# ScalarE takes over the normalising of rows in phases 1 to 3 of an eight-block transformer kernel; a late product is moved by one chunk, and the last result goes out in two halves

## What is computed

```
x = x + tanh(g_xattn[0]) * L0_xattn(layernorm(x), ctx)     # phase 0: attention without softmax
x = x + tanh(g_ffn[0])   * L0_ffn(layernorm(x))            # phase 1: MoE, 8 experts, top 2, width 256
x = x + tanh(g_xattn[1]) * L1_xattn(layernorm(x), ctx)     # phase 2: one-head attention ("riding heads")
x = x + tanh(g_ffn[1])   * L1_ffn(layernorm(x))            # phase 3: MoE, 16 experts, top 4, width 128
x = x + tanh(g_xattn[2]) * L2_xattn(layernorm(x), ctx)     # phase 4: 16-head attention
x = x + tanh(g_ffn[2])   * L2_ffn(layernorm(x))            # phase 5: slots and a GRU step
x = x + tanh(g_xattn[3]) * L3_xattn(layernorm(x), ctx)     # phase 6: 16-head attention
x = x + tanh(g_ffn[3])   * L3_ffn(layernorm(x))            # phase 7: MoE, 32 experts, top 8, width 64

def _layernorm(x, axis=-1, eps=1e-05):
    m = jnp.mean(x, axis=axis, keepdims=True)
    v = jnp.var(x, axis=axis, keepdims=True)
    return (x - m) / jnp.sqrt(v + eps)
```

## Time and profile before

| engine | busy us | share | instructions |
|---|---|---|---|
| TensorE products | 821.9 | 95% | 4427 |
| TensorE weight loads (beside the products) | 558.9 | 65% | 4427 |
| VectorE | 519.4 | 60% | 1446 |
| GpSimd | 471.3 | 55% | 449 |
| ScalarE | 405.5 | 47% | 729 |

### The profile page before, as it was taken

How to read it: one execution, slowest core, us unless ns; L and a number is a source line. 1 busy time by engine, 2 the same in 40 slices (tenths; PEclk the granted TensorE clock), 3 DMA queues, 4 the chain that set the end, 5 groups by cost and what they waited for, 6 DMA issues and landing times. The chain is left out here.

```text
span 861.6 us, 13585 instructions
## 1 busy us (share of the span) xinstructions
PE 821.9 (95%) x4427; PEld 558.9 (65%) x4427; DVE 519.4 (60%) x1446; ACT 405.5 (47%) x729; POOL 471.3 (55%) x449
## 2 busy tenths in 40 slices
PE   5999999998899999999998999999999999999997
PEld 5876676665667666665665666666665576666664
DVE  6866645594765737235545868686856748556431
ACT  2443354634536242334767676756565663424231
POOL 5585756466672646575545444353555366565452
PEclk9899999999999999999999999999999999999999
DMA  8303110314313232332234141412123141424251
GB/s 317 100 21 99 49 50 11 107 43 155 111 38 123 74 122 76 124 122 49 72 93 117 28 108 26 112 29 71 40 60 75 25 146 56 149 69 148 76 157 45
DMA packets 44727, 75.29 MB, mean 87 GB/s; under 512 B 8977, under 2 KB 9361, under 8 KB 44529
## 3 DMA queue, kind: packets, MB, share of 16 engines
q1 hardware_dynamic: 44512, 74.42, 28.5%
q10 hardware_dynamic: 144, 0.01, 0.0%
HBM read 56.11 MB, written 1.51 MB: 67 GB/s over the span
## 5 line engine op out<-in xcount | busy, mean ns | idle before, releaser
L1178 POOL TENSOR_TENSOR shared<-shared,bcs 128x512 f32<-128x512 f32 x192 | 247.4, 1292 | 204.0 <-DVE shared L1214 186.7
L1214 DVE TENSOR_TENSOR shared<-shared,B 128x512 f32<-128x512 f32 x204 | 139.6, 687 | 205.5 <-PE B L862 158.8
L1066 ACT ACTIVATE shared<-B 128x512 f32<-128x512 f32 x204 | 121.6, 598 | 273.7 <-PE B L862 273.2
L935 PE MATMUL Y<-shared,down_lo 128*128 128x512 f32 x408 | 208.3, 596 | 0.0
L1723 POOL TENSOR_TENSOR shared_r<-shared_r,const 128x512 fp32r<-128x512 f32 (+1 forms) x128 | 116.5, 940 | 87.2 <-PE B L1483 69.7
L1782 DVE TENSOR_REDUCE mxh<-B 128x4 fp32r<-128x512 f32 (+1 forms) x128 | 78.8, 617 | 78.4 <-PE B L1483 77.6
L1660 ACT COPY shared<-B 128x512 f32<-128x512 f32 (+1 forms) x128 | 64.7, 505 | 61.7 <-PE B L1502 61.7
L1650 ACT ACTIVATE shared<-B 128x512 f32<-128x512 f32 (+1 forms) x128 | 69.6, 543 | 51.1 <-PE B L1489 49.8
L935 PEld LDWEIGHTS Y<-shared,down_lo 128*128 128x128 f32 x408 | 72.2, 189 | 21.1 <-issue 9.5
L860 PE MATMUL B<-shared_r,gate_hi 128*128 128x512 f32 x102 | 80.9, 794 | 0.0
L860 PE MATMUL B<-x_lo_r,gate_hi 128*128 128x512 f32 x102 | 76.2, 747 | 0.4 <-ACT shared L1066 0.4
(11 more groups left out here) (311 smaller groups left out, 1472.0 us busy)
## 6 DMA issues: line engine op xcount, KB each, us to landing
bcs<-wrow SPq DMA_DIRECT2D x96, 256.0 KB, 3.6
shared_r<-shared_r SPq DMA_DIRECT2D x256, 64.0 KB, 2.0
bcs<-wrow SPq DMA_DIRECT2D x128, 128.0 KB, 2.9
gate_lo<-in_moe SPq DMA_DIRECT2D x9, 256.0 KB, 5.4
up_lo<-in_moe SPq DMA_DIRECT2D x9, 256.0 KB, 5.7
down_lo<-in_moe SPq DMA_DIRECT2D x9, 256.0 KB, 4.6
small<-in_small SPq DMA_DIRECT2D x1, 1372.5 KB, 11.7
X<-in_x SPq DMA_DIRECT2D x4, 256.0 KB, 5.2
```

The source lines that it names most:

```text
L935: nc.tensor.matmul(Y[:], w_raw[2][:, at:at + P], hid[(n0 + c) % HIDDEN], start=(i == 0), stop=(i == m["NC"] - 1))\
L1066: nc.scalar.activation(sg[(n0 + n) % ACTIVE], B[n % GATES][:], ACT.Silu).then_inc(sem("sg_ready"), 1)
L1178: gp.tensor_tensor(hid[(n0 + n) % HIDDEN], hid[(n0 + n) % HIDDEN], bcs[(PLACE.k0[p] + r // m["PER"]) % BROADCAST], ALU.mult)\
L1214: nc.vector.tensor_tensor(hid[(n0 + n) % HIDDEN], sg[(n0 + n) % ACTIVE], up[:], ALU.mult)\
```

## The change

1. In `STREAMS[0]` ScalarE normalises the rows of the MoE steps: Identity activations with scale = rstd and bias = offset, tiles 0 and 1 three chunks behind the statistics, tiles 2 and 3 four chunks behind. GpSimd's L1163 is left only in phase 7.
2. The riders' `apply` moves from VectorE to ScalarE, at the same d=3.
3. For both, VectorE writes the negated means as well, and GpSimd multiplies them with rstd behind its power (`offset`, `offset2`).
4. The riders' `out` and `update` move from d=12 to d=13, and on VectorE the riders' steps of a chunk now stand in front of the MoE statistics.
5. The last result is done in two halves of 256 columns on ScalarE, TensorE (two PSUM banks), VectorE and in the store.

```diff
@@ norm_stats
+            if negate:
+                nc.vector.tensor_scalar(neg_mean[:], mv[:, :, 0], -1.0, None, ALU.mult)
             nc.vector.tensor_scalar(var[:], mv[:, :, 1], LN_EPS, None, ALU.add).then_inc(sem("var_ready"), 1)
@@ RIDE
-            pe={1: ("k",), 2: ("v",), 4: ("xt",), 5: ("q",), 6: ("score",), 10: ("turn",), 11: ("av",), 12: ("out",)},
-            act={1: ("k",), 4: ("xt",), 5: ("q",), 7: ("exp",), 10: ("turn",)},
-            dve={0: ("stats",), 2: ("v",), 3: ("apply",), 6: ("max",), 8: ("norm",), 11: ("add_q",), 12: ("update",)},
+            pe={1: ("k",), 2: ("v",), 4: ("xt",), 5: ("q",), 6: ("score",), 10: ("turn",), 11: ("av",), 13: ("out",)},
+            act={1: ("k",), 3: ("apply",), 4: ("xt",), 5: ("q",), 7: ("exp",), 10: ("turn",)},
+            dve={0: ("stats",), 2: ("v",), 6: ("max",), 8: ("norm",), 11: ("add_q",), 13: ("update",)},
@@ ride_act
+            elif what == "apply":
+                act.wait_ge(sem("ride_offset"), g + 1)
+                for j in range(GB):
+                    ins = nc.scalar.activation(xr[:, tiles(j)], token_tile(g, j), ACT.Identity,
+                                               bias=offset2[:, j:j + 1], scale=rstd2[:, j:j + 1])
+                ins.then_inc(sem("ride_xhat"), 1)
@@ ride_dve
+                v.tensor_scalar(neg_mean2[:], mv2[:, :, 0], -1.0, None, ALU.mult)
-            elif what == "apply":
-                dve.wait_ge(sem("ride_rstd"), g + 1)
-                for j in range(GB):
-                    ins = v.tensor_scalar(xr[:, tiles(j)], token_tile(g, j), mv2[:, j, 0:1], rstd2[:, j:j + 1],
-                                          ALU.subtract, ALU.mult)
-                ins.then_inc(sem("ride_xhat"), 1)
@@ ride_pool
                 gp.tensor_tensor(rstd2[:], var2[:], minus_half[:], ALU.pow).then_inc(sem("ride_rstd"), 1)
+                pool.wait_ge(sem("ride_rstd"), g + 1)
+                gp.tensor_tensor(offset2[:], neg_mean2[:], rstd2[:], ALU.mult).then_inc(sem("ride_offset"), 1)
@@ stream_act
+            def apply(s, js):
+                act.wait_ge(sem("offset_ready"), s)
+                for j in js:
+                    ins = nc.scalar.activation(xhat[s % 2][:, j * P:(j + 1) * P], token_tile(s % NG, j), ACT.Identity,
+                                               bias=offset[:, j:j + 1], scale=rstd[:, j:j + 1])
+                if GB - 1 in js:
+                    ins.then_inc(sem("xhat_ready"), 1)
...
+                if run is STREAMS[0] and n in (3, 4):
+                    apply(run.step(1), (0, 1) if n == 3 else (2, 3))
+                for late in (3, 4) if run is STREAMS[0] else ():
+                    H = run.hook("stats", n - late)
+                    if H is not None and run.step(H) + 2 < LAST:
+                        apply(run.step(H) + 2, (0, 1) if late == 3 else (2, 3))
...
-                result_act(act, 7, LAST - 1)
+                act.wait_ge(sem("y_ready"), LAST)
+                act.wait_ge(sem("yt_ready"), LAST - 1)
+                for h in range(2):
+                    cols = slice(2 * h * P, 2 * (h + 1) * P)
+                    nc.scalar.activation(ysb[:, cols], Y[:, cols], ACT.Identity, bias=ybias[:, 7:8],
+                                         scale=tgate[:, 7:8]).then_inc(sem("last_ysb"), 1)
@@ stream_pool
+                if run is STREAMS[0]:
+                    pool.wait_ge(sem("rstd_ready"), s + 2)
+                    gp.tensor_tensor(offset[:], neg_mean[:], rstd[:], ALU.mult).then_inc(sem("offset_ready"), 1)
             def apply(s, js):
+                if run is STREAMS[0]:
+                    return
@@ stream_dve
+                for g, what in run.rides("dve", n):
+                    ride_dve(dve, st, g, what)
                 H = run.hook("stats", n)
                 if H is not None and run.step(H) + 2 < LAST:
-                    norm_stats(st, (run.step(H) + 2) % NG)
-                for g, what in run.rides("dve", n):
-                    ride_dve(dve, st, g, what)
+                    norm_stats(st, (run.step(H) + 2) % NG, run is STREAMS[0])
@@ the end: SyncE, TensorE, VectorE
+            for h in range(2):
+                sp.wait_ge(sem("last_x"), h + 1)
+                c = slice(((NG - 1) * GB + 2 * h) * P, ((NG - 1) * GB + 2 * h + 2) * P)
+                sp.dma_start(out_d[:, c], X[:, c]).then_inc(sem("stored"), 16)
...
+            for h in range(2):
+                pe.wait_ge(sem("last_ysb"), h + 1)
+                for j in (2 * h, 2 * h + 1):
+                    ins = nc.tensor.transpose((T, B[0])[h][:, tiles(j)], ysb[:, tiles(j)], ident)
+                ins.then_inc(sem("last_yt"), 1)
...
-            finish_dve(dve, NG - 1, LAST)
+            for h in range(2):
+                dve.wait_ge(sem("last_yt"), h + 1)
+                x = X[:, ((NG - 1) * GB + 2 * h) * P:((NG - 1) * GB + 2 * h + 2) * P]
+                nc.vector.tensor_tensor(x, x, (T, B[0])[h][:, 2 * h * P:2 * (h + 1) * P], ALU.add).then_inc(sem("last_x"), 1)
```

More of the change, by code:

```diff
@@ L195, in build @@
         rstd = sb("rstd", [P, GB])
+        neg_mean = sb("neg_mean", [P, GB])
+        offset = sb("offset", [P, GB])
         minus_half = sb("minus_half", [P, GB])
@@ L229, in context, with norm_stats @@
             return CT[:, g * TG + j * P:g * TG + (j + 1) * P:step]
-        def norm_stats(st, g):
+        def norm_stats(st, g, negate=False):
             for j in range(GB):
@@ L560, in build @@
         k2, q2, v2, pr2, pn2, pt2, aq2, xr, xr_t = (area1.tile([P, TG]) for _ in range(9))
-        mx2, nb2, rs2, ri2, var2, rstd2 = (sb(n, [P, GB]) for n in ("mx2", "nb2", "rs2", "ri2", "var2", "rstd2"))
+        mx2, nb2, rs2, ri2, var2, rstd2, neg_mean2, offset2 = (
+            sb(n, [P, GB]) for n in ("mx2", "nb2", "rs2", "ri2", "var2", "rstd2", "neg_mean2", "offset2"))
         mv2 = sb("mv2", [P, GB, 2])
@@ L1198, in stream_dve @@
             if run is STREAMS[0]:
-                norm_stats(st, 1)
+                norm_stats(st, 1, True)
                 pieces = iter(())
@@ L2052, in _ @@
                 moe_sp(sp, 7, g)
-            for g in range(NG):
+            for g in range(NG - 1):
                 sp.wait_ge(sem("x_updated"), LAST - NG + 1 + g)
@@ L2056, in _ @@
                 sp.dma_start(out_d[:, c], X[:, c]).then_inc(sem("stored"), 16)
-            sp.wait_ge(sem("stored"), 16 * NG)
+            for h in range(2):
+                sp.wait_ge(sem("last_x"), h + 1)
+                c = slice(((NG - 1) * GB + 2 * h) * P, ((NG - 1) * GB + 2 * h + 2) * P)
+                sp.dma_start(out_d[:, c], X[:, c]).then_inc(sem("stored"), 16)
+            sp.wait_ge(sem("stored"), 16 * (NG + 1))
         @block.gpsimd
@@ L2112, in _ @@
             pe.wait_ge(sem("x_updated"), LAST - 1)
-            pe.wait_ge(sem("ysb_ready"), LAST)
-            for j in range(GB):
-                ins = nc.tensor.transpose(T[:, j * P:(j + 1) * P], ysb[:, j * P:(j + 1) * P], ident)
-            ins.then_inc(sem("yt_ready"), 1)
+            for h in range(2):
[3 more added lines that the diff above has]
+                ins.then_inc(sem("last_yt"), 1)
         @block.vector
```

## The result

The changed kernel takes 851.8 us (median of 4 runs, 849.3 to 853.8) against 863.2 us: a ratio of 0.988, interval 0.985 to 0.991. The prediction said 849.8 us, range 846.8 to 857.5. The profiled execution took 851.25 us (span 849.5) where that of before took 863.39 (span 861.6), 12.1 us less instead of 13.6. The ratio lies clear of the 0.5% that a measurement can tell, though the gain is under 2%.

A forecast was written before the change was run, and what follows sets the result against it. TensorE's work was taken as the kernel's length, its waits as removable: 5.7 (riders' transposes) + 4.3 (last products) + 3.2 (clock) + 0.4 (tail) = 13.6 us, so 863.4 - 13.6 = 849.8 us, range 846.8 to 857.5.

The forecast's parts named there:

- What bounds the kernel: TensorE, busy 821.9 of 861.6 us, sets the length; its waits in phases 1 to 3 can go.
- Part 1: Riders' normalising on ScalarE: TensorE's waits at their transposes shrink from 6.1 us by 5.7.
- Part 2: GpSimd's new 128x4 multiply for the offset: 0.2 us each, upper end 1.03, no cost to the kernel.
- Rival A: Third rider's offset comes 4 us late from GpSimd's queue, ScalarE is held; 855.3 us, chance 0.20.
- Part 4: Riders' last product one chunk on: waits of 4.8 us shrink by 4.3, 0.55 stays at the third.
- Part 5: Both stretches at 1.2 GHz behind the two long waits go, 1.6 us each, 3.2 us in all.
- Part 6: Last result in halves at the kernel's end: 0.4 us saved, ends 0.15 and 0.6.
- Rivals B and C: B: MoE-step Silus held behind the offset, 867.8 us, chance 0.06. C: waits return at other products, 859.7, 0.07.
- the 3.0 us of room: At the MoE tiles, a Silu ending at 298.51 is needed by its gate product only at 301.53.
- VectorE's new negations ... Nothing: 12 small VectorE instructions, none ahead of a product TensorE waits for: cost 0, or 1 us if one slips.

The follow-up runs named there:

- e1: Kernel before with only the riders' normalising moved to ScalarE, with its negated mean and offset; 856.05 us, ratio 0.994.
- e3: Changed kernel with the MoE norm put back on GpSimd, tile by tile; 853.26 us, ratio 0.990.
- e4: Kernel before with only the MoE norm tiles moved to ScalarE; 862.27 us, ratio 1.000.
- e6: Changed kernel with the last product and update of the third and fourth rider yet one chunk later; 851.52 us in one execution.
- e9: Changed kernel with the last three weight splits of phase 3 one or two chunks later; 849.25 us in one execution.
- e8: Changed kernel with five extra activations, each waited for, ahead of the third rider's tiles on ScalarE; 858.46 us in one execution.
- e2: Kernel before with only the riders' last product and update one chunk on, ahead of VectorE's MoE statistics; 859.82 us, ratio 0.996.
- e7: Changed kernel with two extra activations, each waited for, ahead of the third rider's tiles on ScalarE; 853.53 us in one execution.
- e11: The kernel of e9 again, timed in rounds against the kernel before; 851.35 us, ratio 0.989.

## Why the prediction was right, and what it missed

- **What bounds the kernel.** Right. TensorE's products are the same, and the time went where its waits were named.
- **Part 1, the riders' rows.** 5.7 us expected, 5.95 found. At the third rider 0.2 us was to be left and 0.21 is. The reason was not quite the one given. The transposes stand 1.64 us earlier than before; in before's time ScalarE was free at 196.60 as expected (196.62), but the offset was ready at 196.68, not 196.0. The activations, 1.65 instead of 1.85 us, made that good.
- **Part 2, GpSimd's multiply.** 0.2 us expected, 0.20 and 0.27 found; the upper bound of 1.03 could go. Rival A had its mechanism right: e1 shows it at 1.1 us. The removed tiles keep it away, as the argument against it said; e3 puts 1.4 us on them. e4 shows a second way in which they act, by which of GpSimd's long instructions stand beside VectorE's.
- **Part 4, the last product.** 4.3 expected, 4.55 found; 0.55 left over expected, 0.58 found, and e6 and e9 give it back (0.68 and 0.69).
- **Part 5, the clock.** 3.2 expected, 3.2 found. e8 shows for the third rider's transposes that the wait is the cause, and e2 shows that the second fall goes with the wait for the last product.
- **Part 6, the tail.** 0.4 expected, 0.56 found, inside its ends of 0.15 and 0.6. Both terms held: the last issue ends 846.70 + 0.81 - 845.09 = 2.42 us behind the activation's start, where it was 2.64, so 0.22 earlier (0.15 to 0.26 expected), and the remaining 0.3 lies behind it, in the transfer of half the bytes (up to 0.35).
- **Rivals B and C.** ScalarE waits 3.3 us for GpSimd at the MoE tiles and TensorE feels none of it, so the 3.0 us of room held. No other product of the stream began to wait.
- **The step that failed**, though the forecast held within its range, is "VectorE's new negations ... Nothing". The instructions do cost nothing, but what they write to needs room, and I did not price where that was taken: 0.86 us in the stream and 0.56 in phase 7, 1.4 us of the 1.5 that the profiled execution fell short. The rest balances, by luck: the steps gave 0.6 us more than the sum, phases 4 to 6 another 0.6 by the place of their low clock, the start took 1.18.

What stays open: how the placement acts. That the products run evenly slower when the work tensors are shifted by 32 bytes a partition is shown; by which access, and whether another shift would do the same, was not tried. Nor is it settled whether the long stretch at the start is more frequent with the change (4 of the 10 traces of kernels made from it, 0 of the 4 others), or only fell so. In 8 of the 14 traces the ninth chunk is 0.8 us longer: there TensorE waits some 0.6 us for a setup step of VectorE (L508 in e2) at its first transposes. Both kinds of kernel have it, and what decides it wasn't tried.

## What to carry to other kernels

Where one engine is at 95%, price each of its waits from the start of the product that could have run, look at the granted clock behind the long ones in their own trace, and follow the one queue that feeds the new owner of the work: here these gave 13.6 us against 14.2 found at the places named. Then compare the traces product by product in stretches that the change doesn't touch: an even loss there is not a wait. Here it was the place of two new small tensors, so try a kernel with them behind the large ones. One profiled execution had up to 2.4 us of luck in its start and the 14 traces differ by up to 2.7 in phases 4 to 6, so a difference of that size needs repeated runs and a stretch of the trace to itself.

## What the runs showed of the hardware

- Two tensors of 16 bytes a partition placed ahead of the work tensors made each chunk of phase 7 8 ns longer (153.69 to 154.25 us over 67 steps), and moving them behind took it back (153.68).
- In the stream of phases 1 to 3, waits of TensorE of 1.2, 1.4 and 1.9 us left the granted clock at 1.00 (e7, e3, e4); with waits of 2.6, 3.4, 3.7 and 4.3 us it fell to 1.2 GHz for 3.4 us (before, e1, e4; e8; before; e2). In phases 4 to 6 a wait of 1.6 us was followed by a fall in 10 of 14 traces and not in the other 4, so the length of the wait alone doesn't decide it.
- A VectorE normalising of 128 columns took 0.33 us alone, 0.43 to 0.48 beside a GpSimd norm tile, 1.34 to 1.57 beside one long GpSimd instruction and 2.90 beside two (before, e4).
- The same program started with 3.4 us at 1.2 GHz in one execution and with 10.2 in another (e9, e11); their first gate products lie 2.4 us apart.
- A GpSimd multiply of 128x4 takes 0.20 us where the power of the same shape takes 1.03.
